# Attention stage of a fused decoder layer: all eight key heads multiplied as high and low parts, and the next block's first scores issued one slot later

## The chip, the cores and the metric

The program runs on one core of one Trainium2 chip. The metric is the device time of one execution in microseconds (us); three runs of the kernel before gave 2684.85 us as their median (2683.07 to 2694.03). A profiled execution of the same kernel took 2678.68 us.

The names of the engines are those of the profile: PE (TensorE, with PEld for its weight loads), DVE (VectorE), ACT (ScalarE), POOL (GpSimd) and SP (SyncE, which here issues every transfer).

## The reference, cut to what matters

The layer is a gated feed-forward part with a selection, a cross-attention, and a quantized linear layer, each with a residual and a layer norm. The change touches the attention alone:

```python
# 16 sequences, 112 queries each, 375 keys; 32 query heads, 8 key/value heads, 32 columns a head
q = (query @ Wq).reshape(b, sq, 32, 32).transpose(0, 2, 1, 3)
k = (key @ Wk).reshape(b, sk, 8, 32).transpose(0, 2, 1, 3)
v = (value @ Wv).reshape(b, sk, 8, 32).transpose(0, 2, 1, 3)
k = jnp.repeat(k, 4, axis=1)
v = jnp.repeat(v, 4, axis=1)
scores = jnp.einsum('bhqd,bhkd->bhqk', q, k) * 32 ** -0.5
probs = jax.nn.softmax(scores, axis=-1)
out = jnp.einsum('bhqk,bhkd->bhqd', probs, v)
```

Everything is fp32. The kernel gets fp32 accuracy out of single-pass fp32r matmuls by splitting a factor into a high part (a rounded copy) and a low part (what the rounding left).

## The kernel before

The program runs five passes one behind the other: context (keys and values), gated (the feed-forward part), query, attend, finish. The change is inside `attend_pass`.

`attend_pass` has a block for each of the 16 sequences n. A block has 8 key heads h and, for each, 3 tiles of 125 keys, so 24 slots x = 3h + t. In each slot PE does up to three things, in this order:

- `scores(n, x)`: one matmul that gives scores with keys on the partitions, minus the row maxima. The maxima come in as two extra rows of `qs` (`nm_hi`, `nm_lo`). ACT takes the exponential of the result into the tile `e`.
- `values(g, i)`: for the head three back (`LAG = 3`, g counts heads over all blocks), a third of the product of probabilities and values. For a split head a slot has 2 of its 6 matmuls: three with `e_hi`, then three with `e_lo`. The first one with `e_lo` is in the second slot (i = 1), so x = 3h + 10 for head h. The one head in `FULL` is multiplied unsplit, one fp32 matmul of `e` a slot.
- `first_pair(n', y)`: two matmuls that give plain scores of a later block with queries on the partitions, only for the row maxima; DVE reduces them. A block needs 16 pairs, and `PAIR_AT` says in which slot each stands. Negative entries and entries past a block's start are counted from the start of the block before the one the pair is for: -2 is slot 22 of the block before that.

When the 16 maxima are there, `turn_maxima` (slot `TURN_AT`) transposes them on PE. ACT makes `nm_hi`, DVE `nm_lo`, and SP stores both as rows of `qs` (`put_max`). `scores(n + 1, 0)` waits for these two transfers.

The high part of a head is made by ACT (`HI_ACT`) or DVE (`HI_DVE`), one slot after the head's last exponential. The low part is made by POOL (`LO_POOL`), in the order of the heads; POOL also makes the low part of one piece of Wo in each of the first eight blocks (`split_w`, before head 6). There are 4 buffers of `e`, and 3 each of `e_hi` and `e_lo`.

Each engine runs its list in order, and the lists are written out by hand: there is no planner. In DVE's list the maxima of a slot stand ahead of the high part that is made in that slot (lines 1333 to 1336).

Of the kernel before, what the change touches and what calls it, by code (L numbers as in the profile page):

```python
# [459 lines left out]
def gated_pass(nc, x_t, w_gu, w_d, w_d_tail, ident_f, ident_b, y_dram):  # L460

    FULL = MI_FULL
    MIX = FULL
    UP = FULL + 1
    DOWN = 2 * FULL + 1
    CC = MI // 2
# [7 lines left out]
    with ExitStack() as ctx:  # L476
# [33 lines left out]
        def rows(t):  # L510
            return P if t < FULL else TAIL

# [20 lines left out]
        def muls(g, t):  # L533

            return MI * g + (2 if t == FULL else t if t < 2 else t + 1) + 1

# [520 lines left out]
def attend_pass(nc, kd, vd, qd, w_o, wo_hi, wo_lo, ident_f, od, rd):  # L1057
# [7 lines left out]
    KR = STACK + 2  # L1065
    LAG = 3
    NX, NPAIR = KV * KT, H // 2
    PAIR_AT = (-2, -1, 0, 1, 2, 4, 5, 6, 7, 8, 10, 11, 12, 13, 14, 16)
    PAIR_OF = {x: y for y, x in enumerate(PAIR_AT)}
    TURN_AT = 18  # L1070
    RECIP_AT = 20
    FULL = (3,)
    HI_ACT = (1, 2, 4)
    HI_DVE = tuple(h for h in range(KV) if h not in HI_ACT + FULL)
    LO_POOL = tuple(h for h in range(KV) if h not in FULL)
    NE, NHI, NLO, NO = 4, 3, 3, 3
# [2 lines left out]
    def upto(heads, g):  # L1079

        return len(heads) * (g // KV) + sum(h <= g % KV for h in heads)

    with ExitStack() as ctx:
# [43 lines left out]
        def await_hi(eng, g):  # L1127
            if g % KV in FULL:
                eng.wait_ge(exped, KT * (g + 1))
            elif g % KV in HI_ACT:  # L1130
                eng.wait_ge(hi_act, upto(HI_ACT, g))
            else:
# [6 lines left out]
        def _(sp):  # L1139
# [17 lines left out]
            def put_max(n):  # L1157
                p = n % 2
                sp.wait_ge(nml, n + 1)
                for row, src in ((STACK, nm_hi), (STACK + 1, nm_lo)):  # L1160
                    sp.dma_start(qs[p][row:row + 1].bitcast(F32).rearrange("o f j m q -> o (f j m) q"),
                                 src[:].bitcast(F32)).then_inc(nm_put, 16)
# [12 lines left out]
            def put_recip(c):  # L1175
                sp.wait_ge(recip, c + 1)
                for b in range(GB):
                    n = GB * c + b
                    sp.dma_start(rd.rearrange("h j t -> (h j) t")[:, n * S:(n + 1) * S],
                                 den[c % 2][b * H:(b + 1) * H, :]).then_inc(r_stored, 16)  # L1180
# [11 lines left out]
            for n in range(B):  # L1192
                for h in range(KV):
# [10 lines left out]
                    if h == RECIP_AT // KT and n % GB == 0 and n > 0:  # L1204
                        put_recip(n // GB - 1)
                    if h == TURN_AT // KT and n + 1 < B:
                        put_max(n + 1)
# [31 lines left out]
        def _(act):  # L1239
# [17 lines left out]
            def split_hi(g):  # L1257
                act.wait_ge(exped, KT * (g + 1))
                if g >= NHI:
                    act.wait_ge(pv, g - NHI + 1)  # L1260
                nc.scalar.copy(e_hi[g % NHI][:], e[g % NE][:]).then_inc(hi_act, 1)
# [13 lines left out]
            for n in range(B):  # L1275
                for x in range(NX):
                    h, t = divmod(x, KT)
                    g = KV * n + h
                    exp(n, x)
                    if t == 0 and g >= 1 and (g - 1) % KV in HI_ACT:  # L1280
                        split_hi(g - 1)
                    if t == 1 and g - LAG - 1 >= 0:
                        take(g - LAG - 1)
                    if x == KT * W_SPLIT_AT + 2 and n < KV:
                        split_w(n)
                    if x == TURN_AT + 1 and n + 1 < B:
                        max_hi(n + 1)
# [4 lines left out]
        def _(dve):  # L1292
# [33 lines left out]
            max_lo(0)  # L1326
            for x in range(NX + PAIR_AT[0], NX):
                for pair in pairs_at(-1, x):
                    maxima(*pair)
            for n in range(B):  # L1330
                for x in range(NX):
# [5 lines left out]
                    if x == RECIP_AT and n % GB == 0 and n > 0:  # L1337
                        invert(n // GB - 1)
                    if x == TURN_AT + 2 and n + 1 < B:
                        max_lo(n + 1)  # L1340
# [4 lines left out]
        def _(pe):  # L1345
# [52 lines left out]
            turn_maxima(0)  # L1398
            for x in range(NX + PAIR_AT[0], NX):
                for pair in pairs_at(-1, x):  # L1400
                    first_pair(*pair)
            for n in range(B):
                for x in range(NX):
# [4 lines left out]
                    for pair in pairs_at(n, x):  # L1408
                        first_pair(*pair)
                    if x == TURN_AT and n + 1 < B:  # L1410
                        turn_maxima(n + 1)
# [310 lines left out]
```

## Time and profile before

| what | value |
|---|---|
| median of 3 runs | 2684.85 us |
| the profiled execution | 2678.68 us |
| its span | 2676.9 us |
| PE busy in the span | 2435.1 us (91%) |
| POOL busy in the span | 1357.3 us (51%) |
| DVE busy in the span | 1254.2 us (47%) |
| ACT busy in the span | 1026.1 us (38%) |
| first scores of the attend pass on PE | starts at 1984.5 us |
| first low part on POOL | starts at 2011.0 us |
| last low part on POOL | ends at 2423.8 us |

The shares of the span are means over five passes with different limits. For this change only the stretch from about 1984 to 2426 us counts, and in it what each engine waits for. A start in the trace is in us from the span's start. The busy time of a row that says x5 is that of five instructions in a run.

### The profile page before, as it was taken

To read this page: it belongs to the slowest core of one execution; us is meant where nothing else is said; L and a number is where in the kernel's file an instruction comes from. 1 tells how busy PE (TensorE), PEld (TensorE's weight loads), DVE (VectorE), ACT (ScalarE), POOL (GpSimd) and SP (SyncE) were. 2 spreads that over 40 slices of the span, in tenths; PEclk is the share of its full clock that TensorE was granted. 3 is DMA by queue.
4 is the path that set the end of the run, shared out by engine and by line. 5 is a ranking of instruction groups with operands and counts; after the bars stand their busy time and mean duration, and the time that the engine had idled before them with its cause. 6 is when DMAs were issued, how large, how long until landed. Compare 5 with 4: busy or idle time off the path is not lost. (4 is left out here: it accounts for less than half of the span.)

```text
span 2676.9 us, 32314 instructions
## 1 busy us (share of the span) xinstructions
PE 2435.1 (91%) x12640; PEld 2107.6 (79%) x12640; DVE 1254.2 (47%) x1654; ACT 1026.1 (38%) x1507; POOL 1357.3 (51%) x611
## 2 busy tenths in 40 slices
PE   7999699999999999999999999749979888985998
PEld 7999699978999888998889988749856666654775
DVE  4762104950029610167200783065338778762665
ACT  2111135532336323372333633121107777772111
POOL 5433345844548645467454683230008988883221
PEclk9999799999999999999999999969979999997999
DMA  5555422323322234222243232366556776646673
GB/s 202 180 172 173 172 95 95 110 85 125 125 95 102 100 102 142 96 101 99 94 150 103 97 112 81 112 194 172 151 128 179 185 180 170 161 127 164 157 173 103
DMA packets 228521, 359.10 MB, mean 134 GB/s; under 512 B 107184, under 2 KB 163504, under 8 KB 227664
## 3 DMA queue, kind: packets, MB, share of 16 engines
q1 hardware_dynamic: 228368, 357.02, 44.1%
q8 instruction: 101, 1.65, 0.3%
q14 instruction: 52, 0.43, 0.1%
HBM read 277.57 MB, written 78.70 MB: 133 GB/s over the span
## 5 line engine op out<-in xcount | busy, mean ns | idle before, releaser
L689 POOL TENSOR_TENSOR gp_w_lo<-gp_raw,gp_w_hi 128x1024 fp32r<-128x1024 f32 (+2 forms) x268 | 642.2, 2398 | 602.8 <-ACT gp_w_hi L596 602.4
L58 PE MATMUL gp_acc<-gp_x_hi,gp_w_hi 128*128 128x448 f32 x1376 | 513.1, 373 | 25.4 <-POOL gp_w_lo L689 19.4
L59 PE MATMUL gp_acc<-gp_x_lo,gp_w_hi 128*128 128x448 f32 x1376 | 504.6, 367 | 0.0
L60 PE MATMUL gp_acc<-gp_x_hi,gp_w_lo 128*128 128x448 f32 x1376 | 503.9, 366 | 0.0
L1235 POOL TENSOR_TENSOR ap_e_lo<-ap_e,ap_e_hi 125x1344 fp32r<-125x1344 f32 x112 | 341.6, 3075 | 80.9 <-DVE ap_e_hi L1312 49.9
L596 ACT CAST gp_w_hi<-gp_raw 128x1024 fp32r<-128x1024 f32 (+2 forms) x268 | 273.2, 1022 | 213.1 <-PE gp_acc L60 164.3
L58 PEld LDWEIGHTS gp_acc<-gp_x_hi,gp_w_hi 128*128 128x128 f32 x1376 | 260.0, 189 | 47.2 <-issue 19.5
L58 PE MATMUL gp_acc<-gp_h_hi,gp_w_hi 128*128 128x448 f32 (+1 forms) x704 | 272.2, 387 | 20.0 <-POOL gp_w_lo L689 14.6
L334 DVE TENSOR_REDUCE gp_sel_unit<-gp_keys 112x4 f32<-112x2048 f32 x4 | 9.1, 2286 | 589.5 <-ACT gp_keys L609 589.5
L60 PEld LDWEIGHTS gp_acc<-gp_x_hi,gp_w_lo 128*128 128x128 f32 x1376 | 259.8, 189 | 21.0
L59 PEld LDWEIGHTS gp_acc<-gp_x_lo,gp_w_hi 128*128 128x128 f32 x1376 | 260.2, 189 | 18.9
L1298 DVE TENSOR_REDUCE ap_n_max<-ap_p_s 112x2 f32<-112x750 f32 x256 | 234.3, 938 | 72.3 <-PE ap_p_s L1356 71.2
L59 PE MATMUL gp_acc<-gp_h_lo,gp_w_hi 128*128 128x448 f32 (+1 forms) x704 | 262.2, 372 | 0.0
L60 PE MATMUL gp_acc<-gp_h_hi,gp_w_lo 128*128 128x448 f32 (+1 forms) x704 | 261.8, 372 | 0.0
L1254 ACT ACTIVATE ap_e<-ap_p_t 125x448 f32<-125x448 f32 x384 | 204.1, 544 | 101.8 <-PE ap_p_t L1371 99.4
L1356 PE MATMUL ap_p_s<-ap_ks,ap_qs 96*112 96x376 f32 x512 | 144.2, 367 | 49.6 <-DMA ap_ks<-k_scratch 32.5
L327 DVE TENSOR_SCALAR_CACHE_REDUCE gp_keep<-gp_keys,gp_sel_bound 112x2752 bf16<-112x2752 f32 (+1 forms) x56 | 158.2, 2867 | 63.9 <-ACT gp_keys L609 61.7
L191 POOL TENSOR_TENSOR cp_c_lo<-cp_c_raw,cp_c_hi 128x1504 fp32r<-128x1504 f32 x32 | 110.5, 3477 | 146.6 <-ACT cp_c_hi L160 146.6
L1371 PE MATMUL ap_p_t<-ap_qs,ap_ks 98*125 98x448 f32 x384 | 160.4, 418 | 6.8 <-ACT ap_e L1254 4.1
L58 PEld LDWEIGHTS gp_acc<-gp_h_hi,gp_w_hi 128*128 128x128 f32 (+1 forms) x704 | 136.5, 194 | 36.9 <-POOL gp_w_lo L689 16.8
L1356 PEld LDWEIGHTS ap_p_s<-ap_ks,ap_qs 96*112 96x112 f32 x512 | 91.1, 189 | 93.2 <-DVE ap_n_max L1298 34.1
L615 ACT ACTIVATE gp_act<-gp_acc 128x448 f32<-128x448 f32 x84 | 45.6, 543 | 282.4 <-PE gp_acc L60 282.4
(154 smaller groups left out, 4553.2 us busy)
## 6 DMA issues: line engine op xcount, KB each, us to landing
gp_raw<-in_w_gu SPq DMA_DIRECT2D x172, 512.0 KB, 3.2
gp_raw<-in_w_d SPq DMA_DIRECT2D x80, 512.0 KB, 3.4
cp_c_raw<-in_ctx_t SPq DMA_DIRECT2D x32, 750.0 KB, 6.5
q_scratch<-qp_q_out SPq DMA_DIRECT2D x64, 224.0 KB, 2.6
ap_qs<-q_scratch SPq DMA_DIRECT2D x32, 448.0 KB, 4.8
o_scratch<-ap_o_ab SPq DMA_DIRECT2D x64, 224.0 KB
ap_vs<-v_scratch SPq DMA_DIRECT2D x16, 773.4 KB
k_scratch<-cp_k_out SPq DMA_DIRECT2D x16, 752.0 KB
```

Of the source, the lines that this page charges most:

```text
L58: nc.tensor.matmul(out, wh, xh, start=first, stop=False)
L59: nc.tensor.matmul(out, wh, xl, start=False, stop=False)
L60: return nc.tensor.matmul(out, wl, xh, start=False, stop=last)
L191: nc.gpsimd.tensor_tensor(c_lo[p][:, ks(h), :], c_raw[p][:, ks(h), :], c_hi[p][:, ks(h), :].bitcast(F32), ALU.subtract).then_inc(lo_done, 1)
L327: self.nc.vector.tensor_scalar(self.keep[:, b, 0:width], self.keys[:, b, 0:width], bound[:, b:b + 1], None, op, ALU.add, accum_out=self.co ...
L596: last = nc.scalar.copy(o, i)
L689: last = nc.gpsimd.tensor_tensor(o, i, hi.bitcast(F32), ALU.subtract)
L1235: nc.gpsimd.tensor_tensor(e_lo[g % NLO][:], e[g % NE][:], e_hi[g % NHI][:].bitcast(F32), ALU.subtract).then_inc(lo_pool, 1)
L1254: nc.scalar.activation(e[g % NE][:, x % KT, :], p_t[x % 2][0:KN, 0:T], ACT.Exp, scale=SCALE).then_inc(exped, 1)
L1298: nc.vector.reduce_max(n_max[:, h // 4, 2 * a:2 * a + 2, h % 4], p_s[y % 2][:, :, 0:C], AX_X).then_inc(maxed, 1)
L1356: last = nc.tensor.matmul(p_s[y % 2][:, i, 0:CP], qs[p][0:STACK, half, 2 * a + i, h % 4, :], ks[p][0:STACK, half, h % 4, :], start=True, s ...
L1371: nc.tensor.matmul(p_t[x % 2][0:KN, 0:T], ks[p][0:KR, h // 4, h % 4, t * KN:(t + 1) * KN], qs[p][:, h // 4, :, h % 4, :], start=True, stop ...
```

## The change

```diff
-    PAIR_AT = (-2, -1, 0, 1, 2, 4, 5, 6, 7, 8, 10, 11, 12, 13, 14, 16)
+    PAIR_AT = (-1, 0, 1, 2, 3, 5, 6, 7, 8, 9, 11, 12, 13, 14, 15, 17)
     PAIR_OF = {x: y for y, x in enumerate(PAIR_AT)}
-    TURN_AT = 18
+    TURN_AT = 19
     RECIP_AT = 20
-    FULL = (3,)
-    HI_ACT = (1, 2, 4)
+    FULL = ()
+    HI_ACT = (1, 2, 4, 6)
     HI_DVE = tuple(h for h in range(KV) if h not in HI_ACT + FULL)
     LO_POOL = tuple(h for h in range(KV) if h not in FULL)
```

Head 3 is now split like the others. ACT makes the high parts of heads 1, 2, 4 and 6 (before 1, 2, 4), DVE those of 0, 3, 5 and 7 (before 0, 5, 6, 7), and POOL makes eight low parts a block (before seven). Every pair, and the transpose of the maxima, stands one slot later.

POOL's list, from the start of the pass to the third piece of Wo (`wo_lo`), before:

```order
L1218 MEMSET ap_ks 2x3008 x2
L1235 TENSOR_TENSOR ap_e_lo<-ap_e,ap_e_hi 125x1344 x5
L1223 TENSOR_TENSOR wo_lo<-ap_wo_raw,wo_hi 128x1024
L1235 TENSOR_TENSOR ap_e_lo<-ap_e,ap_e_hi 125x1344 x7
L1223 TENSOR_TENSOR wo_lo<-ap_wo_raw,wo_hi 128x1024
```

And now:

```order
L1218 MEMSET ap_ks 2x3008 x2
L1235 TENSOR_TENSOR ap_e_lo<-ap_e,ap_e_hi 125x1344 x6
L1223 TENSOR_TENSOR wo_lo<-ap_wo_raw,wo_hi 128x1024
L1235 TENSOR_TENSOR ap_e_lo<-ap_e,ap_e_hi 125x1344 x8
L1223 TENSOR_TENSOR wo_lo<-ap_wo_raw,wo_hi 128x1024
```

Between two pieces of Wo there is one low part more.

DVE's list over one block, from the `nm_lo` that ends the maxima of a block (L1302) to the next. L1298 is the maxima of a pair, L1312 a high part. Before, the high parts are those of heads 6, 7, 0 and 5:

```order
L1302 SCALAR_TENSOR_TENSOR ap_nm_lo<-ap_p_s,ap_nm_hi 32x112
L1312 TENSOR_SCALAR ap_e_hi,ap_e_sum<-ap_e 125x1344
L1298 TENSOR_REDUCE ap_n_max<-ap_p_s 112x2 x3
L1312 TENSOR_SCALAR ap_e_hi,ap_e_sum<-ap_e 125x1344
L1298 TENSOR_REDUCE ap_n_max<-ap_p_s 112x2 x2
L1312 TENSOR_SCALAR ap_e_hi,ap_e_sum<-ap_e 125x1344
L1298 TENSOR_REDUCE ap_n_max<-ap_p_s 112x2 x11
L1312 TENSOR_SCALAR ap_e_hi,ap_e_sum<-ap_e 125x1344
L1302 SCALAR_TENSOR_TENSOR ap_nm_lo<-ap_p_s,ap_nm_hi 32x112
```

And now, with the high parts of heads 7, 0, 3 and 5:

```order
L1302 SCALAR_TENSOR_TENSOR ap_nm_lo<-ap_p_s,ap_nm_hi 32x112
L1298 TENSOR_REDUCE ap_n_max<-ap_p_s 112x2 x2
L1312 TENSOR_SCALAR ap_e_hi,ap_e_sum<-ap_e 125x1344
L1298 TENSOR_REDUCE ap_n_max<-ap_p_s 112x2 x3
L1312 TENSOR_SCALAR ap_e_hi,ap_e_sum<-ap_e 125x1344
L1298 TENSOR_REDUCE ap_n_max<-ap_p_s 112x2 x7
L1312 TENSOR_SCALAR ap_e_hi,ap_e_sum<-ap_e 125x1344
L1298 TENSOR_REDUCE ap_n_max<-ap_p_s 112x2 x4
L1312 TENSOR_SCALAR ap_e_hi,ap_e_sum<-ap_e 125x1344
L1302 SCALAR_TENSOR_TENSOR ap_nm_lo<-ap_p_s,ap_nm_hi 32x112
```

Between the high part of head 7 (its list place is slot 0 of the next block) and that of head 0 (slot 3) stand three maxima where two stood.

ACT's list around the transposed maxima of the first block. L1254 is an exponential, L1268 takes a finished head out of PSUM, L1272 is the high part of a piece of Wo, L1244 is `nm_hi`. Before:

```order
L1254 ACTIVATE ap_e<-ap_p_t 125x448 x3
L1268 COPY ap_o_ab<-ap_p_o 66x448
L1244 ACTIVATE ap_nm_hi<-ap_p_s 32x112
L1254 ACTIVATE ap_e<-ap_p_t 125x448
L1272 CAST wo_hi<-ap_wo_raw 128x1024
L1254 ACTIVATE ap_e<-ap_p_t 125x448 x2
L1268 COPY ap_o_ab<-ap_p_o 66x448
```

And now, with L1261 the high part of head 6:

```order
L1254 ACTIVATE ap_e<-ap_p_t 125x448 x3
L1268 COPY ap_o_ab<-ap_p_o 66x448
L1254 ACTIVATE ap_e<-ap_p_t 125x448
L1272 CAST wo_hi<-ap_wo_raw 128x1024
L1244 ACTIVATE ap_nm_hi<-ap_p_s 32x112
L1254 ACTIVATE ap_e<-ap_p_t 125x448
L1261 CAST ap_e_hi<-ap_e 125x1344
L1254 ACTIVATE ap_e<-ap_p_t 125x448
L1268 COPY ap_o_ab<-ap_p_o 66x448
```

`nm_hi` now stands behind the copy of the piece of Wo, in the eight blocks that have one.

## Rows read from the trace of the kernel before

**Rows 1.** The page's first part: busy us and share of the span, by engine.

```profile
PE 2435.1 (91%) x12640; PEld 2107.6 (79%) x12640; DVE 1254.2 (47%) x1654; ACT 1026.1 (38%) x1507; POOL 1357.3 (51%) x611
```

**Rows 2.** Stretches: length, busy PE, PEld, DVE, ACT, POOL, clock, DMA share, GB/s.

```profile
2100.45:2126.32 25.87, 22.91 (x106) 16.03 (x105) 20.79 (x26) 20.07 (x38) 23.74 (x9) 1.00 0.72 186
...
2284.78:2310.70 25.92, 22.93 (x106) 16.06 (x105) 20.81 (x26) 19.37 (x37) 21.37 (x8) 1.00 0.68 165
2310.70:2338.28 27.58, 24.50 (x106) 17.18 (x105) 20.86 (x26) 19.36 (x37) 21.32 (x7) 0.94 0.62 157
...
2390.32:2425.80 35.48, 27.52 (x110) 15.19 (x109) 11.67 (x16) 25.69 (x51) 33.39 (x11) 0.97 0.21 48
```

**Rows 3.** Groups by line, 1950 to 2500 us: busy us, mean ns | idle before.

```profile
L1235 POOL TENSOR_TENSOR ap_e_lo<-ap_e,ap_e_hi 125x1344 fp32r<-125x1344 f32 x112 | 341.6, 3075 | 80.9 <-DVE ap_e_hi L1312 49.9 <-ACT ap_e_hi L1261 29.5
L1298 DVE TENSOR_REDUCE ap_n_max<-ap_p_s 112x2 f32<-112x750 f32 x256 | 234.3, 938 | 72.3 <-PE ap_p_s L1356 71.2
...
L1312 DVE TENSOR_SCALAR_CACHE_REDUCE ap_e_hi<-ap_e 125x1344 fp32r<-125x1344 f32 x64 | 99.1, 1548 | 32.5 <-ACT ap_e L1254 26.3 <-PE ap_p_o L1384 6.2
...
L1261 ACT CAST ap_e_hi<-ap_e 125x1344 fp32r<-125x1344 f32 x48 | 62.7, 1307 | 0.0
...
L1272 ACT CAST wo_hi<-ap_wo_raw 128x1024 fp32r<-128x1024 f32 x8 | 8.3, 1032 | 0.0
```

**Rows 4.** Timeline of POOL: start us, us, instruction [idle before <- releaser].

```profile
2011.01 9.13 POOL L1235 TENSOR_TENSOR ap_e_lo<-ap_e,ap_e_hi 125x1344 fp32r<-125x1344 f32 x3 [29.38 <-DVE ap_e_hi L1312]
2023.06 6.10 POOL L1235 TENSOR_TENSOR ap_e_lo<-ap_e,ap_e_hi 125x1344 fp32r<-125x1344 f32 x2 [2.92 <-ACT ap_e_hi L1261]
2029.24 2.39 POOL L1223 TENSOR_TENSOR wo_lo<-ap_wo_raw,wo_hi 128x1024 fp32r<-128x1024 f32 x1
2031.71 15.25 POOL L1235 TENSOR_TENSOR ap_e_lo<-ap_e,ap_e_hi 125x1344 fp32r<-125x1344 f32 x5
...
2232.58 9.09 POOL L1235 TENSOR_TENSOR ap_e_lo<-ap_e,ap_e_hi 125x1344 fp32r<-125x1344 f32 x3 [2.01 <-ACT ap_e_hi L1261]
...
2296.34 12.35 POOL L1235 TENSOR_TENSOR ap_e_lo<-ap_e,ap_e_hi 125x1344 fp32r<-125x1344 f32 x4 [2.46 <-DVE ap_e_hi L1312]
2310.70 9.06 POOL L1235 TENSOR_TENSOR ap_e_lo<-ap_e,ap_e_hi 125x1344 fp32r<-125x1344 f32 x3 [2.01 <-ACT ap_e_hi L1261]
...
2390.32 33.52 POOL L1235 TENSOR_TENSOR ap_e_lo<-ap_e,ap_e_hi 125x1344 fp32r<-125x1344 f32 x11 [2.01 <-ACT ap_e_hi L1261]
```

**Rows 5.** Timeline of PE: slots of a split head, then of the unsplit one.

```profile
2308.47 0.37 PE L1371 MATMUL ap_p_t<-ap_qs,ap_ks 98*125 98x448 f32 x1
...
2309.08 0.37 PE L1371 MATMUL ap_p_t<-ap_qs,ap_ks 98*125 98x448 f32 x1
...
2312.65 0.92 PE L1384 MATMUL ap_p_o<-ap_e,ap_vs 125*66 125x448 f32 x2
...
2313.61 0.92 PE L1384 MATMUL ap_p_o<-ap_e,ap_vs 125*66 125x448 f32 x2
```

**Rows 6.** Waits, 2048 to 2424 us: us in total, times, longest.

```profile
PE ap_p_s L1356 <- DMA ap_ks<-k_scratch: 18.7, 13, 2.0
```

**Rows 7.** Timeline: a wait of PE in slot 22; five maxima of DVE in a run.

```profile
2317.36 0.73 PE L1356 MATMUL ap_p_s<-ap_ks,ap_qs 96*112 96x376 f32 x2 [1.60 <-DMA ap_ks<-k_scratch]
...
2326.95 4.47 DVE L1298 TENSOR_REDUCE ap_n_max<-ap_p_s 112x2 f32<-112x750 f32 x5
```

**Rows 8.** Timeline: the row maxima on their way to the last block's first scores.

```profile
2391.95 0.26 PE L1362 MATMUL ap_p_s<-ident_f,ap_n_max 112*32 112x112 f32 x1
...
2393.60 0.26 DVE L1302 SCALAR_TENSOR_TENSOR ap_nm_lo<-ap_p_s,ap_nm_hi 32x112 fp32r<-32x112 f32 x1 [0.47 <-ACT ap_nm_hi L1244]
...
2394.50 0.59 SPq L1161 DMA_DIRECT2D ap_qs<-ap_nm_lo  x1
...
2396.62 0.47 PE L1371 MATMUL ap_p_t<-ap_qs,ap_ks 98*125 98x448 f32 x1 [0.64 <-DMA ap_qs<-ap_nm_lo]
```

**Rows 9.** DMA issues, 2048 to 2400 us: the last number is the median us to landing.

```profile
ap_qs<-ap_nm_lo SPq DMA_DIRECT2D x14, 14.0 KB, 3.3
```

## The prediction

> **What bounds the kernel now.** I read the page's first part, then the stretches block by block, then the groups by line, and last the timelines of POOL, DVE and PE. The first part misleads here: POOL is busy for 51% of the span, PE for 91% [rows 1]. Taken by block of the attend pass it is otherwise. A block takes about 26 us. In it POOL is busy 23.7 us where it also splits a piece of Wo and 21.4 us where it doesn't, DVE 20.8, ACT 20.1 or 19.4, and PE's rows overlap to 22.9 [rows 2]. So POOL is the fullest engine of the attend pass, and it idles for only 2 to 5 us a block. In the last block, which has no pairs, it doesn't idle at all: eleven low parts in a run, 33.52 us, 3.05 each [rows 4].
>
> POOL's idle time before comes in two places. One is ahead of the low part of head 4, about 2 us a block (2.01 ahead of 2232.58, 2310.70 and 2390.32) [rows 4]: that is where head 3, the unsplit one, has no low part. The other, 2.46 us in the late blocks [rows 4], is ahead of the low part of head 7, which waits for DVE.
>
> The whole is a simple account. From the first low part at 2011.01 to the end of the last (2390.32 + 33.52 = 2423.84) are 412.8 us [rows 4]. The 112 low parts [rows 3] take 112 x 3.05 = 341.6. A piece of Wo costs 2.55, from the end of the low part ahead of it (2023.06 + 6.10 = 2029.16) to the start of the next (2031.71) [rows 4]; eight are 20.4. What is left, 50.8 us, is all the idle time that POOL has.
>
> **The change, part by part.**
>
> *The low part of head 3.* 16 more low parts of 3.05 us are 48.8 us on POOL. Of the 50.8 us of idle time 2.0 are left. Nothing in the change makes a low part shorter, so POOL alone sets a floor: first start + 128 x 3.05 + 20.4 = first start + 410.8. The pass can't gain more than 2.0 us, and every us of idle time over 2.0 that POOL keeps makes it slower.
>
> *The unsplit head goes.* Slots of the unsplit head are 0.96 us apart (2312.65 to 2313.61), slots of a split head without a pair 0.61 (2308.47 to 2309.08) [rows 5]. PE saves 3 x 0.35 = 1.05 us a block, 17 us in all. It lies off the path: PE will wait for POOL instead. I count 0.
>
> *The pairs one slot later.* The pair for the block after next waits for its keys, 18.7 us in 13 waits [rows 6], for example 1.60 us ahead of 2317.36 [rows 7]. It stands in slot 22 before and in slot 23 now. In slots paced by POOL, 3.05 / 3 = 1.0 us each against 0.6 to 0.96, it is issued some 2 us later behind the load, so most of these waits go. But that was time of PE, so also 0 on the path, apart from what it does for POOL's feeding below.
>
> *ACT makes the high part of head 6.* ACT gets 1.31 us a block more [rows 3]: 21.4 us in a block of 26 to 27, still under POOL. DVE keeps four high parts. 0 by load.
>
> *The start.* The first block's head 0 waits for its high part on DVE, and that now stands behind one maxima more, 4.47 / 5 = 0.89 us [rows 7]. The first low part starts at about 2011.9: +0.9.
>
> *How well POOL is fed at the block boundary.* This decides the rest. Take a block in which PE stands in slot 22 until the low part of head 4 is done, and call that time 0. POOL then does heads 5 and 6 until 6.1 (8.65 with a piece of Wo), and needs the high part of head 7 by then, and that of the next head 0 by 9.15 (11.7).
>
> The maxima are transposed in slot 19, whose low-part matmul is freed when head 3 is done, at -3.05; behind the slot's own matmuls the transpose stands at about -2.6. From there over `nm_hi` and `nm_lo` to the issue of the second row took 2.55 us (2391.95 to 2394.50) [rows 8], and the distance in slots is the same, so it is issued at -0.05; where a piece of Wo is copied first, 1.03 us later [rows 3]. From issue to PE's use it took 2.12 us in one place (2394.50 to 2396.62) [rows 8], 3.3 in the median to land [rows 9]. So the first scores of the next block start at N = 2.05 to 3.25; PE by itself, after two slots' matmuls with a pair in one, would be there at about 1.7. Its first pair reaches DVE at N + 0.95. From there DVE's list has a maxima (0.89), head 7's high part (1.55), three maxima (2.7) and head 0's high part (1.55) [rows 3, 7]: 6.7 us. Head 0 is ready at N + 7.65, which is 9.7 to 10.9 against 9.15. POOL waits 0.55 to 1.75 us; I take the middle, 1.1. With a piece of Wo it is 10.7 to 11.9 against 11.7, so 0 to 0.2. Before, the list had two maxima there and the slot was free of a pair.
>
> The late boundaries with pairs are the six between blocks 8 and 14: 6 x 1.1 = 6.6. For the eight early ones and the first block's start I add 1.4. POOL's idle time becomes 8.0 us.
>
> **The sum.** The last low part ends at 2011.0 + 0.9 + 410.8 + 8.0 = 2430.7 against 2423.8: 6.9, say 7 us later. The finish pass follows as before. On the profiled execution (2678.68, its span 2676.9 and 1.8 around it) that is 2685.7, 0.26% more. The median of the runs stands 6.2 us over the profiled execution, so the same step gives 2692. By half: the first eight blocks get slower, from 26.2 (2023.06 to 2232.58 in eight) [rows 4] to 24.4 + 2.55 = 26.95, +6; the late ones go to 24.4 + 1.1 = 25.5 from 25.9 or, where PE's clock fell, 27.6, -4; and the last block gets one low part more, +3.05. With the start and the first blocks' transients that is the same sum, within 2.
>
> **A rule to weigh.** In the block from 2310.70 PE waited for keys and its granted clock was 0.94, a stretch at 1.2 instead of 2.4 GHz, and the block took 27.58 us against 25.92 of the one before it [rows 2, 7]. The Trainium skill (TensorE: Matmul & The Clock Gate, HAM oscillation — how this bites in real kernels) says that a wait which recurs in every tile of a loop can throw the clock back to half each time. The trace agrees for single blocks; most had 1.00. What it would make of the time is rival D.
>
> **The rivals.**
>
> A, the forecast: POOL-bound, starved a little at late boundaries. 2687 to 2697. Chance 0.50.
>
> B: POOL is never starved, since PE gets far enough ahead with what it saves. Then 0.9 - 2.0 = -1.1, so 2684, and up to 2687 with a few waits left. For it: the last block ran eleven low parts without a gap. Against it: that block has no maxima on DVE. Chance 0.22.
>
> C, the slower side: the row maxima arrive late at every boundary. Place: `scores(n, 0)`, which waits for the rows; it decides as soon as they land over 1.5 us behind PE's slot 0. With 3.3 us to land or more, and 0.5 us of queueing behind the loads, N is 3.75: POOL waits 2.25 at the six late boundaries and 0.7 at the eight early ones, 13.5 + 5.6 = 19.1, with the start and 2 for the first block, less 2.0: +20, so 2705. For it: the transpose is a slot later and `nm_hi` stands behind the copy of Wo. Chance 0.15.
>
> D, the clock: PE, which now waits for POOL in each head, and for most of the 2.55 us while POOL splits a piece of Wo, falls to 1.2 GHz in every block. It decides once such a wait is as long as the 1.60 us after which the clock was at half [rows 7]. The block that fell took 1.66 us more than its neighbour [rows 2]; over 15 blocks up to 25, less where PE has slack; with A's sum halved, +22, so 2707. Against it: in the last block, POOL-bound already, the clock was 0.97 with its idle tail. Chance 0.10.
>
> E: PE was the bound after all, and its 17 us and the 18.7 us of waits come off: 2649. POOL's account speaks against it, since it would need low parts in less than 3.05 us. Chance 0.03.
>
> **How the numbers follow.** A measurement of this kernel can't tell less than about 0.5%, 13.4 us, from no change. Same is then 2671.4 to 2698.3: nearly all of A (0.48), B (0.22) and a little of C (0.02), 0.72. Slower is the rest of A, C and D: 0.02 + 0.13 + 0.10 = 0.25. Faster is E, 0.03. The time is A's, 2692. For eight in ten the range goes down to B with a few us for the median's own scatter, 2681, and up to C, 2705.
>
> **What would show it.** Right: POOL busy for over 95% from about 2012 to the end of its last low part, 128 of them at 3.05; no idle time ahead of head 4; PE's waits for keys in the pair mostly gone, and waits of PE for POOL's low parts in their place, as the longest in its list; blocks of 27.0 us in the first half and 25 to 26 in the second; what POOL waits for is DVE's high part of head 0. Wrong: low parts shorter than 3.0 us, or the pass ending before 2421 (then the account fails); POOL idle over 20 us in all with PE at a clock of 0.94 in most blocks (D), or with PE waiting for the row of maxima over 1.5 us at each boundary (C).

## The result, and the profile after

| | before | after |
|---|---|---|
| runs | 17 | 17 |
| median, us | 2690.59 | 2697.66 |
| lowest to highest, us | 2683.07 to 2701.96 | 2691.59 to 2707.56 |
| the profiled execution, us | 2678.68 | 2697.66 |

The ratio of after to before is 1.003 (95% interval 1.0018 to 1.0043), some 8 us more. It is a small loss, below what the forecast called measurable (0.5%), and resolved only because there are 17 runs of each.

The profiled execution of before (2678.68) is quicker than each of the 17 timed runs. So the first pair of traces shows 18.5 us between the spans (2676.9 and 2695.4), more than twice the true step. The kernel before was therefore profiled a second time (2688.74 us, span 2687.0, close to the median); that is called the second trace of before.

The page's first part after the change, beside [rows 1]:

```profile
PE 2433.5 (90%) x12627; PEld 2112.7 (78%) x12640; DVE 1248.7 (46%) x1654; ACT 1042.6 (39%) x1523; POOL 1405.5 (52%) x627
```

POOL has 48 us more (1357.3 to 1405.5), which is the 16 low parts. The groups by line of the attend pass, the kernel after, beside [rows 3]:

```profile
L1235 POOL TENSOR_TENSOR ap_e_lo<-ap_e,ap_e_hi 125x1344 fp32r<-125x1344 f32 x128 | 389.4, 3078 | 49.6 <-DVE ap_e_hi L1312 47.8 <-PE ap_p_o L1390 1.1
```

128 low parts. Their mean of 3078 ns counts each to its own end; in a run they start 3.05 apart, as before. The timeline of POOL after (start, duration, and in brackets the idle time ahead and who ended it), beside [rows 4]:

```profile
2014.59 9.09 POOL L1235 TENSOR_TENSOR ap_e_lo<-ap_e,ap_e_hi 125x1344 fp32r<-125x1344 f32 x3 [31.00 <-DVE ap_e_hi L1312]
...
2034.62 2.39 POOL L1223 TENSOR_TENSOR wo_lo<-ap_wo_raw,wo_hi 128x1024 fp32r<-128x1024 f32 x1
2037.09 24.36 POOL L1235 TENSOR_TENSOR ap_e_lo<-ap_e,ap_e_hi 125x1344 fp32r<-125x1344 f32 x8
2061.53 2.38 POOL L1223 TENSOR_TENSOR wo_lo<-ap_wo_raw,wo_hi 128x1024 fp32r<-128x1024 f32 x1
...
2226.50 27.35 POOL L1235 TENSOR_TENSOR ap_e_lo<-ap_e,ap_e_hi 125x1344 fp32r<-125x1344 f32 x9
2256.19 3.06 POOL L1235 TENSOR_TENSOR ap_e_lo<-ap_e,ap_e_hi 125x1344 fp32r<-125x1344 f32 x1 [2.34 <-DVE ap_e_hi L1312]
2260.77 21.31 POOL L1235 TENSOR_TENSOR ap_e_lo<-ap_e,ap_e_hi 125x1344 fp32r<-125x1344 f32 x7 [1.51 <-DVE ap_e_hi L1312]
2282.80 3.07 POOL L1235 TENSOR_TENSOR ap_e_lo<-ap_e,ap_e_hi 125x1344 fp32r<-125x1344 f32 x1 [0.72 <-DVE ap_e_hi L1312]
2286.81 21.29 POOL L1235 TENSOR_TENSOR ap_e_lo<-ap_e,ap_e_hi 125x1344 fp32r<-125x1344 f32 x7 [0.94 <-DVE ap_e_hi L1312]
2309.22 3.10 POOL L1235 TENSOR_TENSOR ap_e_lo<-ap_e,ap_e_hi 125x1344 fp32r<-125x1344 f32 x1 [1.12 <-PE ap_p_o L1390]
2313.24 21.27 POOL L1235 TENSOR_TENSOR ap_e_lo<-ap_e,ap_e_hi 125x1344 fp32r<-125x1344 f32 x7 [0.91 <-DVE ap_e_hi L1312]
...
2389.46 3.08 POOL L1235 TENSOR_TENSOR ap_e_lo<-ap_e,ap_e_hi 125x1344 fp32r<-125x1344 f32 x1 [0.63 <-DVE ap_e_hi L1312]
2393.88 48.51 POOL L1235 TENSOR_TENSOR ap_e_lo<-ap_e,ap_e_hi 125x1344 fp32r<-125x1344 f32 x16 [1.35 <-DVE ap_e_hi L1312]
```

Two regimes stand here. In the early blocks POOL runs through, but for one stop of 1.09 us in the block from 2144.59: from one piece of Wo to the next are 26.90 us (2034.62 to 2061.53). At each of the six late boundaries it stops twice, first ahead of a single low part (head 7), then ahead of head 0 of the next block. The first stop is 0.63 to 2.48 us (mean 1.4), the second 0.91 to 1.51 (mean 1.1).

From the first low part to the end of the last are 2442.39 - 2014.59 = 427.8 us. In the second trace of before they are 421.0 (2013.09 to 2434.06), in the first 412.8.

The waits of the attend pass after (engine, line, what for: us in total, times, longest), beside [rows 6]:

```profile
PEld ap_p_o L1390 <- POOL ap_e_lo L1235: 43.7, 52, 2.0
PE ap_p_o L1390 <- POOL ap_e_lo L1235: 22.7, 31, 1.6
POOL ap_e_lo L1235 <- DVE ap_e_hi L1312: 15.1, 12, 2.5
PE ap_p_t L1371 <- DMA ap_qs<-ap_nm_lo: 14.5, 15, 2.1
PE ap_p_s L1356 <- DMA ap_ks<-k_scratch: 6.2, 11, 1.0
```

PE now waits for low parts. Its waits for keys fell from 18.7 us in 13 to 6.2 in 11 (the second trace of before has 24.5 in 13). New is the row of the maxima: 14.5 us in 15 waits, at every boundary; before it was 2.0 in 4. The windows of some blocks after (busy time of each engine, granted clock, DMA share), beside [rows 2]:

```profile
2037.09:2063.98 26.89, 23.66 (x108) 16.94 (x107) 20.73 (x27) 21.47 (x40) 26.73 (x9) 0.94 0.73 182
...
2144.59:2172.57 27.98, 25.27 (x114) 18.25 (x114) 21.81 (x27) 22.18 (x41) 26.74 (x9) 0.94 0.69 172
...
2339.78:2367.53 27.75, 23.62 (x108) 16.88 (x106) 20.92 (x27) 20.21 (x38) 24.35 (x9) 0.94 0.64 158
...
2393.88:2442.39 48.51, 34.92 (x158) 22.00 (x155) 20.67 (x26) 37.03 (x67) 48.50 (x16) 0.99 0.24 60
```

The granted clock is 0.94 in most blocks, so each of those has a stretch at 1.2 instead of 2.4 GHz. In the early ones POOL's 26.7 us fill the block all the same: taken from one low part of head 4 to the next, the second to the fourth block last 26.88 us each, the first of them at a clock of 0.94 and the other two at 1.00.

### The profile page after: what moved, and what is told of

It is laid out like the page before. It is cut to its first block and busy times, and to the rows that moved or that the text cites. A ratio compares the mean times of both kernels' runs of the same rounds, so it can differ in the third digit from the quotient of the medians.

```text
span 2695.4 us, 32365 instructions
## 1 busy us (share of the span) xinstructions
PE 2433.5 (90%) x12627; PEld 2112.7 (78%) x12640; DVE 1248.7 (46%) x1654; ACT 1042.6 (39%) x1523; POOL 1405.5 (52%) x627
## 5 line engine op out<-in xcount | busy, mean ns | idle before, releaser
L1235 POOL TENSOR_TENSOR ap_e_lo<-ap_e,ap_e_hi 125x1344 fp32r<-125x1344 f32 x128 | 389.4, 3078 | 49.6 <-DVE ap_e_hi L1312 47.8
L1298 DVE TENSOR_REDUCE ap_n_max<-ap_p_s 112x2 f32<-112x750 f32 x256 | 232.6, 937 | 104.0 <-PE ap_p_s L1356 103.1
L1254 ACT ACTIVATE ap_e<-ap_p_t 125x448 f32<-125x448 f32 x384 | 207.0, 544 | 99.4 <-PE ap_p_t L1371 96.5
L1356 PE MATMUL ap_p_s<-ap_ks,ap_qs 96*112 96x376 f32 x512 | 149.1, 378 | 43.3 <-DMA ap_ks<-k_scratch 21.6
L1371 PE MATMUL ap_p_t<-ap_qs,ap_ks 98*125 98x448 f32 x384 | 151.8, 395 | 15.4 <-DMA ap_qs<-ap_nm_lo 14.9
```

The costliest lines, as they stand in the source:

```text
L1235: nc.gpsimd.tensor_tensor(e_lo[g % NLO][:], e[g % NE][:], e_hi[g % NHI][:].bitcast(F32), ALU.subtract).then_inc(lo_pool, 1)
L1254: nc.scalar.activation(e[g % NE][:, x % KT, :], p_t[x % 2][0:KN, 0:T], ACT.Exp, scale=SCALE).then_inc(exped, 1)
L1298: nc.vector.reduce_max(n_max[:, h // 4, 2 * a:2 * a + 2, h % 4], p_s[y % 2][:, :, 0:C], AX_X).then_inc(maxed, 1)
L1356: last = nc.tensor.matmul(p_s[y % 2][:, i, 0:CP], qs[p][0:STACK, half, 2 * a + i, h % 4, :], ks[p][0:STACK, half, h % 4, :], start=True, s ...
L1371: nc.tensor.matmul(p_t[x % 2][0:KN, 0:T], ks[p][0:KR, h // 4, h % 4, t * KN:(t + 1) * KN], qs[p][:, h // 4, :, h % 4, :], start=True, stop ...
```

## The experiments

Two theories stood at the start. The floor: POOL's list of low parts is the path, and the rest follows from its sum. The chain over the boundary: transpose, `nm_hi`, `nm_lo`, the row's transfer, the first scores, the pairs and DVE's list set the length of a block, at the full clock or at half. The stretch given with each kernel is that of its trace, from the first low part's start to the last one's end; ratios are to the kernel before, which ran beside it. A stretch is that of one execution, and the two of the kernel before differ by 8.2 us, so a difference of a few us between two stretches shows nothing by itself.

**The kernel before, once more.** `before_again` is the kernel before, unchanged.

> The kernel before, unchanged, for a second trace. In the first pair of traces the stretch from the first to the last low part on POOL grew from 412.8 to 427.8 us, 15 us, while the ratio of all runs, 1.003, says 8 us. Theory P (POOL's list of low parts is the path, with some 8 to 17 us of idle time at the block boundaries): the stretch is 412.8 to 420 here, the first trace of before being a lucky one. Rival K (PE's clock): blocks in which the granted clock is 0.94 are the long ones, and a longer stretch than 412.8 comes with more of them.

Measured: 2688.74 us, stretch 421.0, 8.2 more than in the first trace and 1.0 above theory P's range. One of its late blocks, as POOL's timeline has it:

```profile
2306.44 12.35 POOL L1235 TENSOR_TENSOR ap_e_lo<-ap_e,ap_e_hi 125x1344 fp32r<-125x1344 f32 x4 [2.88 <-DVE ap_e_hi L1312]
```

This stop is the one ahead of head 7; the one that head 3 leaves ahead of head 4 is 2.0 us, as in [rows 4]. The stop ahead of head 7 is 2.88 to 3.88 us in the six late blocks (mean 3.3). In the first trace it is 2.32 to 4.19 (mean 2.8), so the 2.46 of [rows 4] is one of its smaller values. Of the 8.2 us 2.7 came in these late blocks and 4.7 in the early ones. Rival K's sign came too: by windows from one low part of head 4 to the next, six of 14 blocks have a clock of 0.94 and last 26.7 to 28.1 us, where the first trace has three. POOL's idle time is a property of the execution as well as of the kernel.

**One part of the change each.** `split_only` has the split of head 3 and ACT's fourth high part, with the pairs where they were; `shift_only` the later pairs alone, in the kernel before.

```diff
# split_only, against after (shift_only is the reverse, against before)
-    PAIR_AT = (-1, 0, 1, 2, 3, 5, 6, 7, 8, 9, 11, 12, 13, 14, 15, 17)
+    PAIR_AT = (-2, -1, 0, 1, 2, 4, 5, 6, 7, 8, 10, 11, 12, 13, 14, 16)
-    TURN_AT = 19
+    TURN_AT = 18
```

> Half of the change: no head in FULL, ACT makes the high part of head 6 too, but the pairs and the transpose of the maxima stay in their slots of before. Theory P: POOL has all 128 low parts, so the stretch is 410.8 us plus POOL's idle time. At the boundaries DVE has one maxima less ahead of the high part of head 0 (0.9 us) and the row maxima come a slot earlier, so idle time falls to 5 to 12 us: ratio to before 0.999 to 1.003. Rival S (the shift is what keeps POOL fed, since the waits for keys stand in slot 22 without it): idle time 17 us or more, ratio 1.004 to 1.008.

> The other half: head 3 stays unsplit and ACT has three high parts, but the pairs and the transpose stand one slot later, as in the changed kernel. Theory P: POOL has 112 low parts and is not full, PE's waits for keys (18.7 us in 13) mostly go, the transpose comes after one more unsplit matmul, so the waits for the row maxima grow; sum between -8 and +4 us, ratio 0.997 to 1.0015. Rival S: the waits for keys were time of the path, and the ratio is 0.993 to 0.996.

Measured: `split_only` 2704.49 us, 1.0053 (1.0038 to 1.0068), stretch 433.8; `shift_only` 2699.61, 1.0032 (1.0019 to 1.0045), stretch 431.5. `split_only` came out as rival S had it; `shift_only` is slower than both of its theories allowed. Each alone is slower, and both together (1.003) are no slower than the shift alone. What each waits for, the first two rows from `split_only`, then two from `shift_only`:

```profile
PE ap_p_s L1356 <- DMA ap_ks<-k_scratch: 22.0, 13, 2.1
POOL ap_e_lo L1235 <- DVE ap_e_hi L1312: 21.6, 20, 3.6
```

```profile
PE ap_p_t L1371 <- DMA ap_qs<-ap_nm_lo: 17.2, 15, 2.8
PE ap_p_s L1356 <- DMA ap_ks<-k_scratch: 16.0, 13, 3.3
```

With the split alone the keys are late as before, and POOL, which has no slack left, waits 21.6 us for what comes late behind them. With the shift alone the keys' waits hardly fall (16.0 of 18.7 to 24.5 us), and the row of the maxima comes late on top. Only both together bring the keys' waits down to 6.2 us: PE must also be held back by POOL to come to the keys later. `third_lo`, below, bears this out: with less work on POOL the keys' waits are back at 14.5 us in 13. By the medians beside their own runs of before, the shift is worth 13.9 - 7.1 = 6.8 us to the split kernel and costs the unsplit one 9.0.

The clock has a part in that. In `shift_only` the nine blocks ahead of the last two, taken from one low part of head 4 to the next, alternate between two kinds: five of 28.15 to 28.19 us at a clock of 0.88 and four of 26.43 to 26.45 at 1.00. Two neighbours:

```profile
2300.84:2327.28 26.44, 23.15 (x107) 15.97 (x106) 20.60 (x25) 19.06 (x37) 21.31 (x7) 1.00 0.68 162
2327.28:2355.46 28.18, 25.79 (x107) 18.23 (x106) 20.81 (x25) 19.05 (x37) 21.33 (x7) 0.88 0.62 154
```

PE waits no longer in the second (1.3 us for keys and 0.9 for the row, against 1.1 and 1.1), and the block lasts 1.7 us more. What share of the 9.0 us is the clock's wasn't tested.

**POOL's list made shorter.** `third_lo` makes only the first of three tiles of head 3's low part; the low parts of the other two are left out, so its values are not the reference's. PE's work is unchanged.

```diff
+                    cut = slice(0, 1 if g % KV == 3 else KT)
-                    nc.gpsimd.tensor_tensor(e_lo[g % NLO][:], e[g % NE][:], ...
+                    nc.gpsimd.tensor_tensor(e_lo[g % NLO][:, cut], e[g % NE][:, cut], ...
```

> The changed kernel, but POOL subtracts only the first of three tiles of head 3's low part (the other two are multiplied as they happen to stand in the buffer, so part of the computation is left out): 16 x about 2.0 us less on POOL, nothing else moved. Theory P: in the eight early blocks, where POOL has no idle time, each gets 0.5 to 2.0 us shorter, in the late ones little since what they wait for is DVE and PE at the boundary; -10 to -22 us against the changed kernel, ratio to before 0.995 to 0.999. Rival K (the clock and PE set the blocks): -0 to -5 us, ratio 1.001 to 1.003.

Measured: 2695.82 us, 1.0015 (1.0005 to 1.0025), stretch 424.6. A run of five low parts with a short one is 13.33 us, so the short one takes 13.33 - 4 x 3.05 = 1.13 and POOL has 16 x 1.92 = 30.7 us less to do. Some 3 us of them came back in the stretch (427.8 to 424.6) and 4 by the ratios, whose intervals overlap: rival K's range, not theory P's. And these 3 us stand in the last two blocks. From the first low part to head 0 of block 14 are 379.3 us in after (2014.59 to 2393.88) and 378.9 here (2018.10 to 2396.99), though POOL had 14 x 1.92 = 26.9 us less to do in them. Three neighbouring blocks:

```profile
2061.17:2089.76 28.59, 24.75 (x106) 17.78 (x106) 20.50 (x25) 21.10 (x39) 24.86 (x10) 0.88 0.67 169
2089.76:2116.09 26.33, 22.33 (x106) 15.79 (x106) 20.30 (x25) 21.10 (x39) 24.88 (x9) 1.00 0.75 183
2116.09:2144.16 28.07, 24.96 (x106) 17.92 (x106) 21.26 (x26) 21.10 (x39) 24.88 (x9) 0.88 0.69 173
```

No engine is full: POOL has 24.9 of 26.3 to 28.6 us. At the full clock a block takes 26.33, at 0.88 it takes 28.07 or 28.59, and the mean of the seven from the first piece of Wo to the last (2035.23 to 2225.77) is 27.22, no less than the 26.90 of the floor. So there is a second limit, as high as the first. That it is the chain over the boundary is what the next kernels test.

**The chain over the boundary, link by link,** each against after. `filler` has PE do six matmuls a block whose results nobody reads, three ahead of the wait for keys and three ahead of the wait for the row, and puts these two waits behind the others of their slot. `turn18` puts the transpose back into slot 18. `hi_first` puts DVE's high part ahead of the maxima of its slot.

```diff
# filler, in first_pair; the same in scores ahead of nm_put (arguments and the order of the waits left out)
+                if n >= 2 and y == 0:
+                    for _ in range(3):
+                        nc.tensor.matmul(p_s[0][:, 0, 0:CP], qs[1 - p][...], ks[1 - p][...], start=True, stop=True)
# turn18
-    TURN_AT = 19
+    TURN_AT = 18
# hi_first
-                    for pair in pairs_at(n, x):
-                        maxima(*pair)
                     if t == 0 and KV * n + h >= 1:
                         follow(KV * n + h - 1)
+                    for pair in pairs_at(n, x):
+                        maxima(*pair)
```

> The changed kernel with six matmuls more a block, of the shapes of its neighbours and into a bank that the next real matmul overwrites: three in slot 23 behind all other waits but ahead of the wait for the keys, three in slot 0 ahead of the wait for the row maxima. PE waits there anyway (in the trace of the changed kernel 6.2 us in 11 and 14.5 us in 15). Theory K (the half-clock stretches behind these waits are what makes blocks long: 27.9 to 28.6 us at a clock of 0.88 to 0.94 against 26.3 at 1.00): the granted clock of the stretch of low parts rises from 0.95 to 0.97 or more, and the kernel gets 3 to 10 us faster, ratio to before 0.9995 to 1.002. Theory P (POOL's list and DVE's order are the path, the clock only follows): nothing gained, up to 5 us lost where the waits are shorter than 0.6 us, ratio 1.003 to 1.005.

> The changed kernel with the transpose of the maxima back in slot 18 (the pairs stay where the change put them), so that the new row maxima are stored a slot earlier and nm_hi stands ahead of the copy of Wo on ACT again. PE may wait up to 0.7 us for DVE's last maxima. Theory N (the late row maxima are the wait that starves POOL at the boundary and lets the clock fall): PE's wait for them falls from 14.5 us to under 5, the stretch of low parts from 427.8 to 417 to 423, ratio to before 0.999 to 1.001. Theory P: POOL's list sets early blocks anyway, only the six late boundaries gain 0.5 us each, ratio 1.002 to 1.003.

> The changed kernel, but in a slot where DVE has both a high part and the maxima of a pair, the high part comes first (slots 0, 3, 12): heads 7, 0 and 3 reach POOL up to 0.9 us earlier, the maxima up to 1.5 us later, and PE's next pairs with them. Theory P (POOL waits for DVE's list at the boundary): its idle time falls by 0.9 us at each late boundary, 5 to 6 us in all, ratio 1.0005 to 1.002. Theory N: what comes late is the row maxima ahead of both, so the gain is 0 to 3 us, or a loss by PE's waits for the maxima: ratio 1.002 to 1.004.

> Both edits, transpose in slot 18 and high parts first. If either theory holds its gain is here: ratio 0.998 to 1.001. If POOL's floor of 410.8 us is reached, the stretch can't be under it.

| kernel | median, us | ratio (95%) | stretch | clock in the stretch |
|---|---|---|---|---|
| after | 2697.66 | 1.003 (1.0018 to 1.0043) | 427.8 | 0.95 |
| filler | 2694.15 | 1.0009 (0.9996 to 1.0022) | 424.6 | 0.98 |
| turn18 | 2695.52 | 1.0016 (1.0003 to 1.0029) | 425.5 | 0.96 |
| hi_first | 2694.15 | 1.0006 (0.9992 to 1.0021) | 430.0 | 0.92 |
| turn18_hi_first | 2693.28 | 1.0007 (0.9991 to 1.0022) | 422.0 | 0.96 |

By its ratio each takes back some of the loss, but all their intervals overlap with that of after, so no single one is shown to be the cause. `filler` is in theory K's range, `hi_first` in theory P's, `turn18` between its two, and the pair of edits no better than `hi_first` alone. `filler` raised the clock (0.95 to 0.98 in the stretch) though PE got more to do. `turn18` missed its aim, waits for the row of under 5 us: it is still late at 14 boundaries.

```profile
PE ap_p_t L1371 <- DMA ap_qs<-ap_nm_lo: 13.7, 14, 2.3
PEld ap_p_s L1362 <- DVE ap_n_max L1298: 11.9, 14, 0.9
```

The second row is the transpose, which in slot 18 waits for the last maxima: it can't start much earlier. `hi_first`'s one trace is longer than its ratio suggests (a wait for keys of 4.4 us in it); why isn't known.

**All three together.** `combo` has the three edits above.

> The changed kernel with all three edits: transpose in slot 18, high parts first on DVE, and the six filling matmuls a block. Theory K+P (POOL's 410.8 us are the floor, what lies above is boundary idle time that late rows and a half clock make): the stretch of low parts is 415 to 421 us, clock 0.97 or more, ratio to before 0.997 to 1.000. Rival Q (the gains are one and the same idle time and don't add): ratio 1.0005 to 1.001, as each alone.

Measured: 2687.36 us, 0.9987 (0.9976 to 0.9997), stretch 418.4. POOL's timeline:

```profile
2036.22 24.38 POOL L1235 TENSOR_TENSOR ap_e_lo<-ap_e,ap_e_hi 125x1344 fp32r<-125x1344 f32 x8
...
2224.72 54.88 POOL L1235 TENSOR_TENSOR ap_e_lo<-ap_e,ap_e_hi 125x1344 fp32r<-125x1344 f32 x18
...
2332.47 24.36 POOL L1235 TENSOR_TENSOR ap_e_lo<-ap_e,ap_e_hi 125x1344 fp32r<-125x1344 f32 x8 [1.74 <-DVE ap_e_hi L1312]
...
2383.53 48.56 POOL L1235 TENSOR_TENSOR ap_e_lo<-ap_e,ap_e_hi 125x1344 fp32r<-125x1344 f32 x16 [0.89 <-DVE ap_e_hi L1312]
```

The wait ahead of head 7 is left at one boundary (1.05 us), and POOL idles for 7.6 us over its floor of 410.8. Theory K+P holds and rival Q doesn't. Here POOL is fed as the forecast had it for the change alone (8.0 us of idle time), and against before that is a gain of 1.3 in a thousand. With this list on POOL at most those 7.6 us are left to win in the stretch.

**The floor lowered,** each against `combo`. `combo_wo_dve` has DVE make the low parts of Wo (2.55 us each on POOL); `mixed` leaves head 3 unsplit in the eight blocks that split a piece of Wo, and splits it in the other eight.

```diff
# combo_wo_dve, in DVE's list instead of POOL's
+                    if x == KT * W_SPLIT_AT + 3 and n < KV:
+                        split_w(n)
# mixed; every test of FULL, HI_ACT, HI_DVE and LO_POOL goes by these
+    def full(g):
+        return g % KV == 3 and g // KV < KV
+    def by_act(g):
+        return not full(g) and g % KV in ((1, 2, 4) if g // KV < KV else (1, 2, 4, 6))
```

> As the kernel with all three edits, and DVE instead of POOL makes the low parts of the pieces of Wo (slot 21 of the first eight blocks). POOL's floor falls by 20.4 us to 390.4. Theory P (in early blocks POOL's list is the path): early blocks fall from 26.9 to 24.9 to 26 us, 8 to 16 us in all, ratio 0.992 to 0.997. Theory K (PE's and DVE's chain over the boundary allows no block under about 26.4 either): early blocks 26.3 to 26.9, ratio within 0.002 of the kernel it starts from.

> As the kernel with all three edits, but head 3 stays unsplit in the eight blocks in which POOL also has a piece of Wo, and is split in the eight that follow. POOL's floor is 120 x 3.05 + 20.4 = 386.4 us. Theory P: early blocks 26.2 to 26.5 us instead of 26.95, the late ones as in the kernel it starts from: 4 to 6 us faster than that, ratio 0.995 to 0.999. Theory K: no faster than it, since PE gets 8 x 1.05 us more work and waits for the row maxima at each boundary.

Measured: `combo_wo_dve` 2698.84 us, 1.0034 (1.0021 to 1.0047); `mixed` 2678.26, 0.9957 (0.9941 to 0.9973). `mixed` is quicker than the kernel before and after, and 9 us quicker than `combo`, where theory P had 4 to 6. Its stretch is 411.2 us at a floor of 120 x 3.05 + 20.4 = 386.4; with head 3 off POOL's list the early blocks last 25.8 us ((2209.01 - 2028.36) / 7) instead of 26.9, and four of the six late blocks, with all eight heads split, 24.9 to 25.3 (the other two 27.3, at a clock of 0.94). Leaving head 3 unsplit in the early blocks is what `mixed` has over `combo`. Whether the split is worth anything in the late ones isn't shown: no run has the three edits with head 3 unsplit everywhere. Windows of an early and a late block of it:

```profile
2080.74:2107.05 26.31, 25.20 (x115) 17.37 (x114) 21.38 (x26) 19.66 (x37) 23.77 (x8) 1.00 0.75 184
2271.39:2296.52 25.13, 23.88 (x113) 16.79 (x112) 20.28 (x26) 19.94 (x38) 24.39 (x8) 1.00 0.69 169
```

`combo_wo_dve` missed both of its theories: by the medians it is 11.5 us slower than `combo`. The low part of Wo on DVE (nanoseconds, least, median, most), and an addition of the same size on DVE in the finish pass:

```profile
L1317 DVE TENSOR_TENSOR wo_lo<-ap_wo_raw,wo_hi x8: 2694/2712/6078, 2028.4 to 2220.6; 128x1024 fp32r<-128x1024 f32 x8
L1563 DVE TENSOR_TENSOR fp_num<-fp_num,fp_add x14: 1218/1220/1226, 2452.2 to 2646.0; 128x1024 f32<-128x1024 f32 x14
```

Beside POOL's low parts it takes 2.7 us in five cases and 5.9 to 6.1 in three, and POOL's low parts have a mean of 3118 ns, against 3083 in `combo`. One short case and one long one, with POOL beside them:

```profile
2084.55 2.71 DVE L1317 TENSOR_TENSOR wo_lo<-ap_wo_raw,wo_hi 128x1024 fp32r<-128x1024 f32 x1 [1.09 <-ACT wo_hi L1263]
2086.24 3.99 POOL L1226 TENSOR_TENSOR ap_e_lo<-ap_e,ap_e_hi 125x1344 fp32r<-125x1344 f32 x1
...
2053.90 6.04 DVE L1317 TENSOR_TENSOR wo_lo<-ap_wo_raw,wo_hi 128x1024 fp32r<-128x1024 f32 x1 [1.10 <-ACT wo_hi L1263]
2062.34 3.04 POOL L1226 TENSOR_TENSOR ap_e_lo<-ap_e,ap_e_hi 125x1344 fp32r<-125x1344 f32 x1 [3.48 <-DVE ap_e_hi L1303]
```

In the short case a low part ends on POOL at about 2086.2, DVE is done 1.1 us later, and the low part that POOL started at 2086.24 takes 0.9 us more than usual: one of the two engines stands while the other works. In the long case POOL does the rest of one low part and a whole second one (to 2058.86) before DVE is done 1.1 us later. DVE's maxima and high parts queue behind it, and POOL then waits 3.48 us for the high part of head 7. Behind each of the three long ones there is such a stop, and those blocks last 28.8 to 30.4 us. This trace is of the quickest run (2688.52 us), and its stretch, 421.7, is only 3.3 us over that of `combo`; where the rest of the 11.5 goes in a typical run no trace shows.

**The clock by itself.** `filler_before` has the six matmuls in the kernel before.

> The kernel before with the six filling matmuls a block: three in slot 22 ahead of the wait for the keys (18.7 to 24.5 us of waits in 13), three in slot 0 ahead of the row maxima (waits of 2 us in all, so these three cost PE up to 0.6 us a block there). Theory K (the half clock behind a wait costs the block its 1.3 us): clock of the stretch 0.98 or more, ratio 0.997 to 1.000. Theory P: the six matmuls cost what they take in slot 0, ratio 1.000 to 1.003.

Measured: 2694.10 us, 1.0014 (1.0002 to 1.0027), stretch 422.7 at a granted clock of 1.00, where the second trace of before has 421.0 at 0.97. POOL waits 30.1 us for DVE and 27.6 for ACT, and PE for keys 18.6 in 13, as before. That is theory P's range. So in the kernel before these matmuls and the full clock together bring nothing; that the matmuls cost what the clock gives back is a reading, since no run has the clock without them. In after, where the key waits are small and the chain from the row to the high part is what POOL waits for, the same matmuls took the ratio from 1.003 to 1.0009, with intervals that just overlap.

## Why the prediction was right, and what cancelled

The forecast was +7 us and no measurable change; it is +8 (+7.1 by the medians). That the forecast said 2692 and the kernel takes 2697.66 is the base: the median of three runs of before was 2684.85, that of 17 is 2690.59.

*POOL's account.* Right, as a floor. The early blocks came out at 26.9 us (forecast 26.95), the last low parts in one run of 48.51 us, no idle time ahead of head 4. But it isn't the only limit: `third_lo` takes 30.7 us off POOL and gains 3. The forecast put the unsplit head's saving on PE at 0; no run takes that saving away by itself, so this term stays untested.

*The size of POOL's idle time before.* Wrong, by 8.2 us. 50.8 us were read from one execution, which was a quick one. In the second trace they are 421.0 - 362.0 = 59.0. Nearly all of the 10.1 us between the two executions is this and a start 2.1 later. The forecast also took 2.46 us for the wait ahead of head 7 in all late blocks, where its own trace has a mean of 2.8.

*How well POOL is fed at the boundary.* The chain is right, its sizes are not. The forecast's 6 x 1.1 = 6.6 us is all that POOL loses until head 0, counted from a POOL that doesn't stop ahead of head 7. Measured, it stops twice: 8.4 us ahead of head 7 in the six late boundaries (2.34 + 0.72 + 1.12 + 1.10 + 2.48 + 0.63) and 6.7 ahead of head 0, 15.1 in all. That the 6.7 are near the 6.6 is chance. The stop ahead of head 7 was left out, though the forecast's own terms (N + 0.95 + 0.89 + 1.55) have that high part ready at 5.4 to 6.6 against the 6.1 at which POOL needs it. The steps that failed are "N = 2.05 to 3.25" and "its first pair reaches DVE at N + 0.95". PE around a late boundary of the kernel after:

```profile
2302.13 0.42 PE L1390 MATMUL ap_p_o<-ap_e_lo,ap_vs 125*66 125x448 f32 x1 [0.59 <-POOL ap_e_lo L1235]
...
2303.65 0.60 PE L1356 MATMUL ap_p_s<-ap_ks,ap_qs 96*112 96x376 f32 x2 [0.49 <-DMA ap_ks<-k_scratch]
2304.81 0.51 PE L1371 MATMUL ap_p_t<-ap_qs,ap_ks 98*125 98x448 f32 x1 [0.56 <-DMA ap_qs<-ap_nm_lo]
...
2305.87 0.83 PE L1356 MATMUL ap_p_s<-ap_ks,ap_qs 96*112 96x376 f32 x2
```

and DVE beside it:

```profile
2306.74 0.94 DVE L1298 TENSOR_REDUCE ap_n_max<-ap_p_s 112x2 f32<-112x750 f32 x1 [1.44 <-PE ap_p_s L1356]
2307.59 1.54 DVE L1312 TENSOR_SCALAR_CACHE_REDUCE ap_e_hi<-ap_e 125x1344 fp32r<-125x1344 f32 x1
...
2311.60 1.54 DVE L1312 TENSOR_SCALAR_CACHE_REDUCE ap_e_hi<-ap_e 125x1344 fp32r<-125x1344 f32 x1
```

N, the first scores behind the release at 2302.13, is 2.68: inside the forecast's 2.05 to 3.25. But PE got there with three short stops in a row (0.59, 0.49, 0.56 us), and the granted clock falls behind them: a pair takes 0.83 us where it took 0.60. So the pair reaches DVE at N + 1.93, a microsecond later than forecast, and head 7's high part is done at 2309.13. POOL had finished head 6 at 2308.10 and starts head 7 at 2309.22.

The boundary ahead of it had the same three stops, of 0.53, 0.84 and 0.50 us, and no fall of the clock; its pair takes 0.50 us and reaches DVE at N + 1.25:

```profile
2277.95 0.60 PE L1356 MATMUL ap_p_s<-ap_ks,ap_qs 96*112 96x376 f32 x2 [0.84 <-DMA ap_ks<-k_scratch]
2279.06 0.47 PE L1371 MATMUL ap_p_t<-ap_qs,ap_ks 98*125 98x448 f32 x1 [0.50 <-DMA ap_qs<-ap_nm_lo]
...
2279.77 0.50 PE L1356 MATMUL ap_p_s<-ap_ks,ap_qs 96*112 96x376 f32 x2
2280.31 0.94 DVE L1298 TENSOR_REDUCE ap_n_max<-ap_p_s 112x2 f32<-112x750 f32 x1 [0.71 <-PE ap_p_s L1356]
```

Over the six late boundaries N is 2.68 to 4.17 (mean 3.2, forecast 2.05 to 3.25), and the pair reaches DVE 1.25 to 2.14 us later (mean 1.6, forecast 0.95). An estimate from these rows divides the 8.4 us so: 3.5 because the first scores come later than the middle of the forecast's range, 1.8 because a pair needs 1.25 us and not 0.95 even at the full clock, 2.3 for the half clock, and the rest in gaps of 0.1.

*The sum.* Two misses of nearly one size cancel: 17.0 us of idle time where 8.0 were forecast, and 59.0 before where 50.8 were read. With the second trace and its own 8.0 the forecast would have said 0.9 + 410.8 + 8.0 - 421.0 = -1.3 us, rival B's number. A kernel that is fed so exists, it is `combo` (7.6 us of idle time), and it is some 4 us quicker than before (0.8 to 6.5 by its interval). So the total was right partly by luck.

*The rivals.* Of C, its wait came: the row of the maxima is late at all 15 boundaries, 14.5 us in all. But only at two of the six late ones is N near C's 3.75 (3.66 and 4.17), and these two hold 4.8 of the 8.4 us ahead of head 7; in the early blocks POOL's list hides most of the wait. Of D, its clock came (0.94 in most blocks), but not its 22 us: most early blocks lie under POOL's floor, where a slow PE costs nothing. Of the list of signs, "waits for keys mostly gone" and "what POOL waits for is head 0's high part" are half right. "Blocks of 25 to 26 in the second half" is wrong: (2389.46 - 2256.19) / 5 = 26.65, where 25.5 was forecast. POOL is busy for 408.5 of the 430.4 us from 2012 on, 94.9% where over 95% was forecast (95.5% from its first low part on). The others are right. Whether the clock would stay up if the row came in time isn't settled: it fell at boundaries with short stops too.

The Trainium skill's page that the forecast weighed (TensorE: Matmul & The Clock Gate, HAM oscillation — how this bites in real kernels) says that a wait in every tile of a loop can throw the clock back to half each time. By that rule alone D would have been the likeliest. The trace of after agrees for the clock in most blocks, though not in all: the two late boundaries shown have stops of the same kind, and the clock fell at one. For the time it agrees only where POOL's list doesn't fill the block.

## What to carry to other kernels

Sum the list of the fullest engine and compare it with the stretch it lies in: its idle time is all that a change can win there, and added work beyond it is loss. Take that idle time from more than one execution, since here it moved by 8 us, as much as the whole effect. Where two limits lie within a few per cent (POOL's list at 26.9, the chain over the boundary at 26.3 to 28.6) lifting either alone shows little (0.6 to 1.6 in a thousand over before are left, of 3); test them together, and pick the split of work by stage, as `mixed` does, instead of one rule for all blocks.

## What the runs showed of the hardware

A subtraction on DVE with two inputs in SBUF (128 x 1024, fp32) takes 2.7 to 6.1 us while POOL works on tensors in SBUF, against 1.22 us for an addition or product of that size while POOL is quiet (`combo_wo_dve`). That was unexpected in size. The Trainium skill (SBUF — State Buffer, Who interferes with whom) says that a DVE instruction with two SBUF inputs contends with a GpSimd instruction that reads SBUF, and that the order of issue decides which one blocks. The trace agrees in the short cases, with a low part of 3.99 us on POOL as the longest, against 3.10 where DVE makes no low part of Wo. In the three long ones a low part that POOL started after DVE's instruction was still done first.

Three stops of PE of 0.5 to 0.6 us within 3 us were followed by a stretch at 1.2 GHz at one boundary of after, and three of 0.5 to 0.8 us at the boundary ahead of it were not. In `shift_only` blocks with equal waits alternated between 0.88 and 1.00. Six matmuls a block whose results nobody reads brought the clock of the stretch from 0.95 to 0.98, and in the kernel before from 0.97 to 1.00.
